# Maxima of two head pairs side by side in two halves of the array's rows

## What is computed

```
q = (layernorm(x) @ w_q.T)    # 8 batches x 56 queries x 128, 16 heads of 8
k = ctx @ w_k.T ; v = ctx @ w_v.T                     # 8 batches x 1500 keys
attn = softmax(q . k * 8**-0.5)                       # by batch, head, query
x = x + tanh(g_xattn) * ((attn @ v) @ w_o.T)
h = layernorm(x)
top 2 of 8 experts from softmax(h @ gate_w.T), weights renormalised
x = x + tanh(g_ffn) * sum_e w_e * down_e(up_e(h) * gelu(gate_e(h)))
```

## Time and profile before

| | us |
|---|---|
| median of 3 runs | 329.39 |
| lowest, highest | 329.34, 331.74 |
| the profiled execution | 331.68 |
| its span in the trace | 329.9 |
| TensorE busy | 288.1 (87%) |
| VectorE busy | 229.3 (69%) |
| ScalarE busy | 187.5 (57%) |
| GpSimd busy | 92.6 (28%) |

### The profile page before, as it was taken

How to read it: one execution, slowest core, us unless ns; L and a number is a source line. 1 busy time by engine, 2 the same in 40 slices (tenths; PEclk the granted TensorE clock), 3 DMA queues, 4 the chain that set the end, 5 groups by cost and what they waited for, 6 DMA issues and landing times.

```text
span 329.9 us, 7978 instructions
## 1 busy us (share of the span) xinstructions
PE 288.1 (87%) x2795; PEld 222.9 (68%) x2795; DVE 229.3 (69%) x430; ACT 187.5 (57%) x380; POOL 92.6 (28%) x108
## 2 busy tenths in 40 slices
PE   0988498999999999999999998966478999999874
PEld 0554486786886886876887886845366878887552
DVE  3498385786786886877778689523262888888874
ACT  1333466757667667667677665364235657775422
POOL 6021404114114114114115100001701346664330
PEclk9999599999999999999999999999559799999979
DMA  5467992494594592692780893000000000000000
GB/s 150 144 143 126 192 232 93 95 223 157 109 220 143 116 243 108 131 242 95 146 229 0 175 253 143 2 0 2 0 0 2 1 0 0 0 1 0 2 0 28
DMA packets 10012, 32.54 MB, mean 99 GB/s; under 512 B 2608, under 2 KB 3120, under 8 KB 9992
## 3 DMA queue, kind: packets, MB, share of 16 engines
q1 hardware_dynamic: 9272, 32.01, 39.4%
q10 hardware_dynamic: 720, 0.27, 0.3%
HBM read 13.26 MB, written 0.23 MB: 41 GB/s over the span
## 4 chain that ended last, share of the span: by engine, by line
PE 67%; DVE 10%; DMA 5%; SPq 5%; ACT 4%; issue 4%; POOL 2%; DVEq 0%; ACTq 0%; POOLq 0%
PE score_ps L871 13%; PE o_ps L905 12%; PE max_ps L891 11%; PE misc_ps L860 5%; SPq L234 5%; PE misc_ps L854 4%; PE score_ps L1097 3%; DMA kx<-k_high 3%; PE score_ps L1098 2%; PE score_ps L1099 2%; ACT probs L478 2%; DVE kx L821 2%; DVE k_low L802 2%; DMA ctx_sb<-in_ctxT 2%; PE max_ps L921 2%
## 5 line engine op out<-in xcount | busy, mean ns | idle before, releaser
L653 DVE TENSOR_REDUCE part_max<-max_ps 112x1 f32<-112x512 f32 (+1 forms) x192 | 118.8, 672 | 46.1 <-PE max_ps L891 43.6
L478 ACT ACTIVATE probs<-score_ps 128x448 f32<-128x448 f32 x192 | 91.7, 544 | 35.8 <-PE score_ps L871 34.2
L871 PE MATMUL score_ps<-qx,kx 104*128 104x224 f32 (+1 forms) x384 | 77.7, 288 | 7.1 <-DMA kx<-kx 5.3
L871 PEld LDWEIGHTS score_ps<-qx,kx 104*128 104x128 f32 (+1 forms) x384 | 67.4, 190 | 21.9 <-issue 13.5
L891 PE MATMUL max_ps<-kx,qx 96*112 96x512 f32 (+1 forms) x192 | 78.3, 413 | 1.6 <-DMA kx<-k_high 0.6
L905 PE MATMUL o_ps<-probs,v_sb 128*32 128x112 f32 (+1 forms) x1536 | 47.8, 262 | 3.2 <-ACT probs L478 3.2
L357 POOL TENSOR_TENSOR k_low<-k_full,k_high 128x512 fp32r<-128x512 f32 (+1 forms) x21 | 26.8, 1277 | 82.6 <-ACT k_full L461 82.6
L905 PEld LDWEIGHTS o_ps<-probs,v_sb 128*32 128x32 f32 (+1 forms) x1536 | 36.3, 109 | 15.4 <-ACT probs L478 9.7
L891 PEld LDWEIGHTS max_ps<-kx,qx 96*112 96x112 f32 x192 | 34.3, 180 | 5.3 <-issue 2.2
L402 POOL TENSOR_TENSOR kx<-gu_sb,kx 128x512 fp32r<-128x512 f32 x16 | 23.1, 1445 | 43.9 <-ACT kx L551 43.9
L585 ACT ACTIVATE kx<-probs 128x448 fp32r<-128x448 f32 x32 | 18.3, 576 | 24.6 <-DVE probs L816 24.1
(11 more groups left out here) (150 smaller groups left out, 381.5 us busy)
## 6 DMA issues: line engine op xcount, KB each, us to landing
kx<-k_high SPq DMA_DIRECT2D x60, 187.5 KB, 3.9
kx<-k_low SPq DMA_DIRECT2D x30, 187.5 KB, 3.9
ctx_sb<-in_ctxT SPq DMA_DIRECT2D x7, 750.0 KB, 6.2
gu_sb<-in_guT SPq DMA_DIRECT2D x8, 512.0 KB, 4.8
dn_sb<-in_dnT SPq DMA_DIRECT2D x8, 256.0 KB, 5.2
ctx_sb<-in_ctxT SPq DMA_DIRECT2D x2, 256.0 KB, 7.4
kx<-k_high SPq DMA_DIRECT2D x4, 123.5 KB, 2.3
kx<-kx SPq DMA_DIRECT2D x3, 96.0 KB
```

The costliest lines, as they stand in the source:

```text
L478: nc.scalar.activation(probs[:, (KT * h + t) % 8, :], score_ps[:, t % 3, 0:SC // 2], ACT.Exp, scale=SCALE).then_inc(exp_done, 1)
L653: nc.vector.reduce_max(part_max[:, p, c:c + 1], max_ps[0:PC, bank, 0:size], AX.X).then_inc(max_taken, turns)
L871: last = nc.tensor.matmul(score_ps[0:m, t % 3, GC * g:GC * g + GC], kx[0:KR, 2 * par + h, g, 128 * t:128 * t + m], qx[0:KR, par, 2 * h + g ...
```

## The change

The rows of `kx`, `q_parts` and `qx` are laid out anew: rows 0 to 15 (`XR`) are the ones and maxima, rows 16 to 63 (`PR` = 48) the first pair of a group with its three parts side by side, rows 64 to 111 the second pair. The product for the maximum of the first pair takes rows 0 to 63, that of the second pair rows 64 to 111, and the two are issued one behind the other into two banks. So six pairs of products stand in a unit in place of twelve products; after which score tiles they stand changes too. Scores take 112 rows instead of 104.

`k_high`, `k_low` and `k_full` become one tensor `k_parts`; a transfer takes 16 rows of all three parts to 48 rows of `kx`, two for each group instead of three. The third part is now `k_full`, which is therefore made for batch 0 too; SP waits for `k_saved` as well. Queries' rests are made by one operation with a mask (`low_mask`) over all 112 rows. The rows of ones are filled by GpSimd for each slot, and the transfers for them go. `rstd` and `ident` come earlier in GpSimd's order. Ahead of everything TensorE makes three products of zeros. In the second half `x_expert_high`, `x_expert_low` and `zeros` lie elsewhere.

```diff
-MR = 96
-KR = MR + 2 * HP
-MOVES = 16 * 3
+XR = 16
+PR = 48
+MR = XR + 2 * PR
+MOVES = 16 * 2
@@ max_product
-    if first and n < HP:
-        return n, 0
+    step, p = n // 2, n % 2
+    if first and step < 2:
+        return 2 * step + p, 0
     if first:
-        return (n - HP) // 2, 1 + (n - HP) % 2
-    return n // NCH, n % NCH
+        return 2 * ((step - 2) // 2) + p, 1 + step % 2
+    return 2 * (step // NCH) + p, step % NCH
@@ move_keys
-            for row, src in ((0, k_high), (1, k_low), (2, k_high)):
-                r = 32 * (2 * h + g)
-                eng.dma_start(kx[32 * row:32 * row + 32, slot, g, start:start + size].bitcast(f32),
-                              src[r:r + 32, start:start + size].bitcast(f32)).then_inc(landed, 16)
+            for p in range(2):
+                r = 32 * (2 * h + g) + 16 * p
+                eng.dma_start(kx[XR + PR * p:XR + PR * p + PR, slot, g, start:start + size].bitcast(f32),
+                              k_parts[r:r + 16, :, start:start + size]).then_inc(landed, 16)
@@ sync
             sp.wait_ge(k_low_saved, 1)
+            sp.wait_ge(k_saved, 2)
@@
             sp.wait_ge(k_low_saved, NCH)
+            sp.wait_ge(k_saved, 2 * NCH)
@@
-            sp.wait_ge(kx_ones, 1)
-            sp.dma_start(kx[MR:KR, 0, 1, :].bitcast(f32), kx[MR:KR, 0, 0, :].bitcast(f32)).then_inc(ones_moved, 16)
             move_unit(0, 1)
-            ones_rows(1)
-            ones_rows(2)
-            ones_rows(3)
@@ gpsimd
-            nc.gpsimd.memset(kx[MR:128, 0, 0, :].bitcast(f32), 1.0).then_inc(kx_ones, 1)
-            pool.wait_ge(kx_ones, 1)
@@ (after ident, third_rows and head_mask; the other masks follow)
+            pool.wait_ge(var_ready, 1)
+            nc.gpsimd.tensor_tensor(rstd[:, :], var_eps[:, :], minus_half[:, :], ALU.pow).then_inc(rstd_ready, 1)
@@
+            def ones_rows(slot):
+                nc.gpsimd.memset(kx[0:XR, slot, :, :].bitcast(f32), 1.0).then_inc(kx_ones, 1)
+
+            ones_rows(0)
@@
             stage(0, 0, 1)
             stage(1, 1, 0)
+            ones_rows(1)
             for n in range(NCH):
                 k_rest(1, n)
+            ones_rows(2)
+            ones_rows(3)
@@ vector, q_rest
-                low = q_parts[64:MR, g, :]
-                nc.vector.tensor_tensor(low, q_banks[g][64:MR, 0:TOK], low.bitcast(f32),
-                                        ALU.subtract).then_inc(q_low_saved, 1)
+                nc.vector.scalar_tensor_tensor(q_parts[:, g, :], q_parts[:, g, :].bitcast(f32), low_mask[0:MR, 0:1],
+                                               q_banks[g][0:MR, 0:TOK], ALU.mult, ALU.add).then_inc(q_low_saved, 1)
@@ tensor, max_scores
                 if n == 0:
                     pe.wait_ge(qx_ready, v + 1)
+                    pe.wait_ge(kx_ones, slot + 1)
@@
-                if not first or n >= 3:
-                    next_bank(turn)
-                nc.tensor.matmul(max_ps[0:PC, bank, 0:size], qx[0:MR, par, 2 * h + p // 2, PC * (p % 2):PC * (p % 2) + PC],
-                                 kx[0:MR, slot, p // 2, start:start + size], start=True, stop=True
-                                 ).then_inc(max_done, turns)
+                if not first or n >= 2:
+                    next_bank(turn + 1)
+                for k, (start, end) in enumerate(((0, XR + PR), (XR + PR, MR))):
+                    p, c = max_product(n + k, first)
+                    begin, size = chunk(c)
+                    nc.tensor.matmul(max_ps[0:PC, (bank + k) % 3, 0:size],
+                                     qx[start:end, par, 2 * h + p // 2, PC * k:PC * k + PC],
+                                     kx[start:end, slot, p // 2, begin:begin + size], start=True, stop=True
+                                     ).then_inc(max_done, turns if k else 1)
@@
+            pe.wait_ge(blank_ready, 1)
+            for _ in range(3):
+                nc.tensor.matmul(misc_ps[:, :], blank[:, 0:128], blank, start=True, stop=True)
             pe.wait_ge(wk_loaded, 16)
@@ attention
                 scores(i, par, h, 0, rows)
                 next_max(6, 0)
                 scores(i, par, h, 1)
-                next_max(7, 1)
                 scores(i, par, h, 2)
+                scores(i, par, h, 3)
                 next_max(8, 2)
-                scores(i, par, h, 3)
-                next_max(9, 3)
+                job(0)
                 denominators(u - 1, 1 - h, ring(u, RUN), RUN % 3)
-                job(0)
                 attend(i, par, h, 0)
@@ (run B: pairs after tiles 4 and 7; run C:)
-                for t in range(2 * RUN, KT):
-                    scores(i, par, h, t)
-                    later_max(t - 6, t + 3)
+                scores(i, par, h, 8)
+                later_max(2, 11)
+                scores(i, par, h, 9)
+                scores(i, par, h, 10)
+                scores(i, par, h, 11)
+                later_max(4, 13)
                 job(2)
```

More of the change, by code:

```diff
@@ L81, in flamingo_block @@
         q_parts = sb("q_parts", [MR, G, TOK], f32r)
-        k_high = sb("k_high", [128, KPAD], f32r)
-        k_low = sb("k_low", [128, KPAD], f32r)
-        k_full = sb("k_full", [128, KPAD])
+        k_parts = sb("k_parts", [128, 3, KPAD])
+        k_high, k_low, k_full = k_parts[:, 0, :].bitcast(f32r), k_parts[:, 1, :].bitcast(f32r), k_parts[:, 2, :]
         ctx_sb = sb("ctx_sb", [128, 2, KPAD])
@@ L139, in flamingo_block @@
         x_low = kx_flat[:, 12 * F + (2 * FT + 1) * TOK:12 * F + (2 * FT + 2) * TOK]
-        x_expert_high = k_high[:, 0:2 * TOK].rearrange("p (a t) -> p a t", a=2)
-        x_expert_low = k_low[:, 0:2 * TOK].rearrange("p (a t) -> p a t", a=2)
-        zeros = k_high[:, 2 * TOK:2 * TOK + 128]
+        qx_flat = qx[:, :, :, :].rearrange("p a g c -> p (a g c)")
+        x_expert_high = qx_flat[:, 0:2 * TOK].rearrange("p (a t) -> p a t", a=2)
+        x_expert_low = qx_flat[:, 2 * TOK:4 * TOK].rearrange("p (a t) -> p a t", a=2)
+        zeros = kx_flat[:, 12 * F + (2 * FT + 2) * TOK:12 * F + (2 * FT + 2) * TOK + 128]
         x_expert = k_full[:, 0:TOK]
@@ L147, in flamingo_block @@
         yT = o_flat[:, 2 * TOK:3 * TOK]
+        blank = k_full[:, 0:CK]
         score_ps = pb("score_ps", [128, 3, 512])
@@ L452, in _, with k_copy @@
             nc.scalar.activation(scratch[:, :], scratch[:, :], ACT.Exp).then_inc(exp_done, FIRST_EXP)
-            def k_copy(b, n, bank, whole=True):
+            def k_copy(b, n, bank):
                 start, size = chunk(n)
                 act.wait_ge(k_done, NCH * b + n + 1)
[L458 to L461, removed]
+                nc.scalar.activation(k_high[:, start:start + size], bank[:, 0:size], ACT.Copy).then_inc(k_saved, 1)
+                nc.scalar.activation(k_full[:, start:start + size], bank[:, 0:size], ACT.Copy).then_inc(k_saved, 1)
             def keys_moved(i, par):
@@ L679, in invert @@
                 nc.vector.reciprocal(inv_den[:, PC * h:PC * h + PC], max_ps[:, bank, 0:PC]).then_inc(max_taken, 1)
+            nc.vector.memset(blank, 0.0).then_inc(blank_ready, 1)
             nc.vector.memset(scratch[:, :], 0.0).then_inc(scratch_ready, 1)
@@ L871, in scores @@
                     last = nc.tensor.matmul(score_ps[0:m, t % 3, GC * g:GC * g + GC],
-                                            kx[0:KR, 2 * par + h, g, 128 * t:128 * t + m],
-                                            qx[0:KR, par, 2 * h + g, :], start=True, stop=True)
+                                            kx[0:MR, 2 * par + h, g, 128 * t:128 * t + m],
+                                            qx[0:MR, par, 2 * h + g, :], start=True, stop=True)
                 last.then_inc(scores_done, 1)
@@ L967, in _ @@
             pe.wait_ge(q_low_saved, 2)
-            for n in range(UM):
-                if n < HP and n % 2 == 0:
+            for n in range(0, UM, 2):
+                if n < HP:
                     pe.wait_ge(kx_begun[n // 2], MOVES)
-                if n >= HP and n % 4 == 0:
+                elif n % 4 == 0:
                     pe.wait_ge(kx_loaded[0][n // 8], MOVES)
@@ L988, in _ @@
             transpose_max(0, UM + 2, 2)
-            for n in range(2, AHEAD):
-                max_scores(0, 0, 1, n, UM + 1 + n, (1 + n) % 3, turns=3 if n == AHEAD - 1 else 1)
+            max_scores(0, 0, 1, 2, UM + 3, 0)
+            max_scores(0, 0, 1, 4, UM + 5, 2, turns=3)
             pe.wait_ge(k_saved, 4 * NCH)
-            pe.wait_ge(ones_moved, 64)
+            pe.wait_ge(consts, 1)
             def attention(i, par, h, rows, jobs=(0, 1, 2), after=True):
@@ L1024, in attention @@
                 scores(i, par, h, 5)
-                next_max(11, 6)
                 scores(i, par, h, 6)
+                scores(i, par, h, 7)
                 later_max(0, 7)
-                scores(i, par, h, 7)
-                later_max(1, 8)
                 job(1)
@@ L1191, with rows_thrice @@
     layout = np.ascontiguousarray
+    def rows_thrice(columns):
+        thrice = np.tile(columns, (1, 1, 1, 3)).reshape(D, G, 2 * PR)
```

(3 more changed lines are left out.)

61 lines of the change are left out of this document (29 added, 32 removed).

## The result

The changed kernel takes 349.25 us (median of 4 runs, 346.72 to 353.56) against 329.37 before: ratio 1.057, 95% interval 1.047 to 1.067, so slower. The forecast was slower, 339 us, with a range of 326 to 349. The profiled execution has a span of 345.0 us, 15.1 more than before. Medians in this document are over all executions of a kernel, of which a few are some per cent slower at a lower granted clock; the ratios leave those out, and stand only where two or more are left.

What follows compares the result with a forecast made beforehand. TensorE was taken to set the attention's pace, with VectorE 2.8 us a unit behind. Attention +17 us (15.5 in 12 loop units, 1.5 in units 12 to 14) and head -7 gave +10 on 329.4: 339 us, range 326 to 349.

Steps and rivals of the forecast that it cites:

- The wait in run A: First TensorE stretch of an attention unit: 0.21 us waiting for a bank VectorE must free, expected to go.
- The price of a pair: Attention, two maxima products between score tiles: 0.71 us, 0.25 more than before, with the array running empty at row changes.
- the first rival: Attention: the second product's weights don't lengthen the pair, +0.15 us a pair, 331 us in all; chance 0.13.
- runs A, B and C: TensorE's three stretches in an attention unit: first to lengthen 0.29 us, the others 0.50 each, 1.29 a unit.
- the signs of error: Listed traces that would show the forecast wrong, among them VectorE's queue (`max_rows`) waiting at the pair behind tile 8.
- the fourth rival: Key moves: transfers from 16 rows slower than from 32; half as long again costs 24 us, 360 in all; chance 0.06.
- The head: Everything up to the attention's steady part: five items summing to -7 us, between -4 and -10.
- (a): Head: the transfers of ones go and the wait behind `k_saved` ends at 33.76 us: -3.4 us.
- (c): Head: first projection at half rate sped by zero products and earlier `rstd`, less extra ScalarE copies: -1 us (+1 to -2.8).
- (e): Head: unit 2's keys can't move before GpSimd has subtracted batch 1, so time is given back: +1 us.
- (d): Head: without the pause, the first unit's first run isn't at 1.2 GHz: -1.4 us.
- two products that don't overlap: Attention: a pair's products don't overlap at all, +0.37 us a pair, 348 us in all; a rival, chance 0.08.

Runs made afterwards that it cites:

- e3_both: Changed kernel with each product of a pair over all 112 rows and three 32-row transfers a group, new order kept: 331.74 us, ratio 1.005.
- e5_order: e3_both with maxima products issued one behind each score tile and the denominators ahead of the job, as before the change: 325.67 us, ratio 0.985.
- e2_moves3: Changed kernel with three transfers a group, one for each part, each reading 32 rows: 336.33 us, ratio 1.022.
- e12_best_again: Same kernel as e6_order_ones, measured again in five rounds: 323.43 us, ratio 0.983.
- e6_order_ones: e5_order with GpSimd filling all four slots' rows of ones before it subtracts batch 1: 322.27 us, ratio 0.976.

## Why the prediction was right and wrong

**The direction and its first cause: right.** The array runs empty at a change from 112 to 64 rows as it does at one from 128 to 16; the load idles 0.11 us before and 0.23 to 0.25 us behind each pair. With transfers of 32 rows the kernel is still slower, 1.022, though part of that is the order. The wait in run A went in every second unit; in the others, where the job is a chunk of keys, the two loads of the denominators idle 0.24 us each instead (108.5 and 108.9 us).

**The price of a pair: 0.71 put, 0.60 measured.** The term that failed is the second weight load, 0.10 us behind the first. I read it off `attend`, whose loads go one after the other into different columns; loads into different rows go together. That was the first rival (+0.15 a pair, chance 0.13), and its sum for runs A, B and C nearly holds in a unit without waits: 4.41, 4.24 and 4.14 us by it from the same unit before (112.08 on), 4.31, 4.23 and 4.12 measured from 118.52 to 131.18. The units gave 12 x 0.57 = 7 us where the forecast had 15.5.

**What it omitted: the order's own price.** I charged the edit of the order only with pairs and credited it with the wait in run A. With equal rows and transfers it costs 0.38 us a unit (e3_both against e5_order), while the halves, in that order, cost 0.32 (e2_moves3 against e3_both), 5.5 us in all by the ratios. That `max_rows` would be a wait stood among the signs of error, without a price.

**The transfers: the fourth rival, chance 0.06, is what decided.** Its place and its mechanism were right: 16 rows are slower than 32, it was to bite from 15% on, and it was 25%. Undoing it alone gives 11.6 us. My argument against it, that bytes are the same and issues fewer, says nothing of the rate. What I had not priced is that each wait can bring a stretch at half clock with it, which two of five did. The step that set the chance was wrong: the row at 123.38 showed half a microsecond of slack in a queue with the exponentials behind it, and the edit touched just that.

**The head: -7 put, -3.3 at the first scores, 0 at unit 2.** (a) happened, and (c) in this execution, by the zero products or by chance. The column's 1.00 on which (c) reads the first microseconds is no reading: the trace of the kernel before has no entry of the clock before 13.6 us, and where a trace has one beside a projection of 2.04 us (e12_best_again) it says 0.50. What failed is (e), the +1 that is given back. The moves of batch 1 start when GpSimd has subtracted, at 31.9 instead of 36.0, and run B of the first unit already needs them for unit 2's maxima; so at most the 4.1 us between those two starts could come through, and with slow transfers they landed at 47.7 instead of 51.3. In e3_both the head gives 3.8 us. (d) failed as well: the clock was 0.50 again from 35.4 to 42.2 us, after TensorE had waited twice for VectorE (0.78 us before 33.40, 0.88 before 35.17).

By these steps the sum of 339 was short by the transfers (+11.6) and by the head (+4.5: unit 2 starts at 61.2 in e2_moves3 against 63.7 before, and the rest up to 63.7 is in the 11.6), and long by the steady units (-8: 12.66 us instead of 13.37). That makes 347; the 2 us to the median I can't put in one place. The median of 349.25 lies 0.25 us above the range that was given, and the forecast's own range, 333 to 344, missed it. That it lies so near the range's end is luck: the range reached 349 for a case that didn't come, two products that don't overlap, and left out the slow transfers that did. Without those the time is 336 us (e2_moves3), close to the forecast, but there too because two errors partly cancel, +4.5 for the head and -8 for the units.

**A version that beats both:** e6_order_ones, measured again as e12_best_again, keeps the layout, the early `rstd` and `ident`, the zero products and GpSimd's fills, and drops row halves, pairs and transfers of 16 rows. It takes 322 to 323 us, 1.7 to 2.4% less than before (intervals 0.967 to 0.984 and 0.977 to 0.989).

## What to carry to other kernels

A stretch of products in another row mode costs about 0.4 us of empty array and open weight loads, and a pair of 512 columns gains back only the 0.21 us of its second product. By these prices such products pay only if several pairs follow each other, which no run here tries. Price a change to a transfer by its rate and by what waits behind its landing, not by its bytes alone. When work is grouped, look for the wait that needs two buffers where one was enough. And before a gain in the head is put down to an edit, look at the same microseconds in the other traces with that edit.

## What the runs showed of the hardware

- Weights for rows 0 to 63 and 64 to 111 load at the same time: 0.17 us for both, and a pair costs the 0.60 us of one product. In the same half the second adds 0.21 us. The Trainium skill, TensorE: Matmul & The Clock Gate, Measured speedup vs the span model, says that a further tile adds some 4 ns; these runs agree: in all 96 pairs of the changed kernel the second product starts 3 or 4 ns behind the first.
- With transfers within SBUF that read 16 rows of three pieces each, a batch moves in 15.6 to 16.2 us (batches begun between 70 and 180 us); with ones that read 32 rows it takes 12.6 to 13.8, whatever their number (4, 8 or 12) and size.
- With a change of mode around every product the granted clock fell below 1.00 in the steady part (0.70 over 120 to 130 us), though the trace has TensorE busy for 10.00 of 10.00 us. Behind each of these products the weight load had stood idle for 0.23 us. In the steady part of the changed kernel the clock was 0.50 for 3.4 us twice, each time behind a wait of TensorE of 0.8 to 0.9 us for ScalarE; a wait of 1.07 us in another unit was followed by none.
- VectorE's cast of 16 x 1024 took 0.77 to 1.43 us in eight traces and 2.57 to 4.30 in six, where it met most of a fill of 2.65 us by GpSimd. In all fourteen traces it ended 0.54 to 0.55 us behind the end of a GpSimd instruction that ran beside it, subtractions included: as if it had stood still until then. A fill that starts under a running cast takes 3.2 us in place of 2.65.
